# A tree of small networks, every leaf for every token, or the tokens sorted by leaf: one layer of an eight-layer kernel

## The reference, cut to what matters

```python
def _fff(x, node_w, node_b, w1, b1, w2, b2):       # once for q, k and v
    for _ in range(DEPTH):                          # DEPTH = 4
        score = einsum('nd,nd->n', xf, node_w[cur]) + node_b[cur]
        cur = 2 * cur + 1 + (score >= 0)
    leaf = cur - N_NODES                            # 0..15
    sel = one_hot(leaf, N_LEAVES)
    hidden_all = relu(einsum('nd,ldh->lnh', xf, w1) + b1[:, None, :])     # h is 64 wide
    hidden = hidden_all * sel.T[:, :, None]
    return einsum('lnh,lho->no', hidden, w2) + sel @ b2
attn = softmax(einsum('bqd,bkd->bqk', q, k) * scale)
out = einsum('bqk,bkd->bqd', attn, v)
```

## Time and profile before

| | us |
|---|---|
| median of 3 runs (1261.86 to 1264.03) | 1263.0 |
| the profiled execution's own time | 1262.16 |
| its span | 1260.3 |
| PE busy in the span | 1066.9 (85%) |
| DVE busy | 633.9 (50%) |
| ACT busy | 518.1 (41%) |
| POOL busy | 182.4 (14%) |

### The profile page before, as it was taken

The page is one execution under the profiler, slowest core; times in us unless marked ns, Lnnn a source line. Parts: engine busy times, 40 slices in busy tenths (PEclk is TensorE's granted clock), DMA queues, the critical chain, the costliest instruction groups (busy, mean ns, idle before and its releaser), DMA issues.

```text
span 1260.3 us, 12073 instructions
## 1 busy us (share of the span) xinstructions
PE 1066.9 (85%) x3752; PEld 460.1 (37%) x3752; DVE 633.9 (50%) x1123; ACT 518.1 (41%) x960; POOL 182.4 (14%) x160
## 2 busy tenths in 40 slices
PE   4898989898899999998847958677778999997677
PEld 2354545444222222222514633222224444442333
DVE  3213131332888778641513434799964555552443
ACT  4322222323367767675303435655552222226510
POOL 9000000000000000000173530366620000000000
PEclk9899999998799999998788979799997999999779
DMA  9600000020021212113013420000000000000001
GB/s 191 214 2 0 0 0 0 0 59 23 20 64 39 64 40 64 39 46 91 11 31 89 135 77 0 1 0 1 0 1 0 1 1 0 0 0 0 1 0 33
DMA packets 60307, 42.13 MB, mean 33 GB/s; under 512 B 17352, under 2 KB 57277, under 8 KB 60164
## 3 DMA queue, kind: packets, MB, share of 16 engines
q1 hardware_dynamic: 57956, 38.80, 11.3%
q0 software_dynamic: 2304, 2.76, 0.7%
HBM read 29.59 MB, written 13.67 MB: 34 GB/s over the span
## 4 chain that ended last, share of the span: by engine, by line
PE 61%; DVE 14%; issue 13%; ACT 8%; SPq 2%; DMA 1%; POOL 1%; DVEq 0%; ACTq 0%; POOLq 0%; another core or an unknown queue 0%
PE psum L566 59%; ACT sb_scr L1256 5%; DVE sb_scr L1736 3%; DVE sb_scr L1986 2%; DVE sb_scr L1995 2%; ACT psum L1256 1%; DVE sb_small L1697 1%; PE psum L1028 1%; SPq L347 1%; PE psum L1010 1%; DVE sb_x L1617 0%; DVE sb_h L1600 0%; ACT L1256 0%; DVE sb_scr L1638 0%; DVE sb_scr L1810 0%
## 5 line engine op out<-in xcount | busy, mean ns | idle before, releaser
L1256 ACT ACTIVATE sb_scr<-psum 128x512 f32<-128x512 f32 (+2 forms) x648 | 323.1, 537 | 491.9 <-PE psum L566 386.7
L566 PE MATMUL psum<-sb_h,sb_wide 128*128 (+1 forms) x448 | 226.4, 612 | 0.0
L1736 DVE TENSOR_REDUCE sb_scr<-psum 128x2 f32<-128x1024 f32 x128 | 154.3, 1223 | 43.7 <-PE psum L566 43.1
L566 PE MATMUL psum<-sb_scr,sb_wide 128*128 128x512 f32 x256 | 132.2, 598 | 6.1 <-DVE sb_scr L2057 6.1
L566 PEld LDWEIGHTS psum<-sb_h,sb_wide 128*128 128x128 f32 x448 | 86.0, 196 | 99.4 <-issue 99.0
L534 POOL DMA_INDIRECT expert_in<-sb_scr x32 | 31.2, 975 | 586.1 <-DVE sb_scr L1881 576.7
L1680 DVE TENSOR_SCALAR sb_scr<-psum,sb_b 128x512 f32<-128x512 f32 x48 | 36.0, 751 | 152.9 <-PE psum L566 152.9
L566 PE MATMUL psum<-sb_kstack,sb_qstack 96*128 96x512 bf16 x256 | 100.9, 406 | 6.4 <-DVE sb_scr L1736 6.0
L1256 ACT ACTIVATE sb_scr<-psum,sb_b 128x512 f32<-128x512 f32 x60 | 40.8, 687 | 159.2 <-PE psum L566 159.2
L566 PE MATMUL psum<-sb_qstack,sb_kstack 128*128 128x512 bf16 x256 | 99.1, 392 | 3.5 <-ACT sb_scr L1256 2.0
L566 PE MATMUL psum<-sb_wparts,sb_pick 96*128 96x512 bf16 (+1 forms) x192 | 66.4, 402 | 39.0 <-DVE sb_scr L1995 28.8
(11 more groups left out here) (222 smaller groups left out, 1299.8 us busy)
## 6 DMA issues: line engine op xcount, KB each, us to landing
sb_qstack<-q_bounce SPq DMA_DIRECT2D x48, 96.0 KB
sb_kstack<-k_bounce SPq DMA_DIRECT2D x144, 32.0 KB
expert_in<-sb_scr SPq DMA_DIRECT2D x4, 645.0 KB, 7.2
sb_scr<-expert_in SPq DMA_DIRECT2D x8, 322.5 KB
expert_out<-sb_scr SPq DMA_DIRECT2D x4, 512.0 KB, 5.9
sb_wide<-L_ffn_W SPq DMA_DIRECT2D x2, 1024.0 KB, 7.4
sb_scr<-expert_out SPq DMA_DIRECT2D x8, 256.0 KB, 4.7
q_bounce<-sb_scr SPq DMA_DIRECT2D x12, 128.0 KB, 2.4
```

Source lines behind the costliest of these rows:

```text
L566: return nc.tensor.matmul(out_, w, r, start=start, stop=stop, **kw)
L1256: return nc.scalar.activation(out_, in_, func, **kw)
L1736: v.reduce_max(headmax[:, g % 2, t:t + 2, j], banks, AX.X).then_inc(sem("maxed"), 1)
```

## The change

The first feed-forward is computed by leaf. Node scores for all 2048 tokens and three trees are taken at once, with tokens on partitions, and DVE works out each token's leaf, its place in a table sorted by leaf (each leaf's block padded to whole tiles of 128, so 32 tiles a tree), and for each tile the leaf it belongs to. POOL scatters the rows of h to the tables `leaf_in` in DRAM (16 indirect transfers a tree). Then 24 chunks of four tiles (8 a tree) go through: SP loads the rows of the chunk (`load_chunk`); SP (three) and ACT (one) load the weights of the tile's leaf, after reading the leaf's number from SBUF into a register (`value_load`); PE turns the rows, multiplies with w1 (64 wide) and with w2 (with b2 as a further row); ACT takes the relu, DVE copies, ACT stores the result to `leaf_out`. The rings of rows, results and weights hold four chunks each. POOL gathers the results back token by token (16 indirect transfers a tree). The attention is then a pipeline over all 16 steps, and the product that turns the probabilities has, in place of the identity, a diagonal matrix of the reciprocal sums (`inv_eye0`). `blank` has a buffer of its own, so the table of the fourth layer is cleared later; the parameter loads share one semaphore; the loops over batches are written out. The parts of the host's data layout: w1, w2, b1 and b2 of a leaf stand in one [128 x 193] block of `tree_rows`.

```diff
-            def trees(b, last):
...
-            with pe.Fori(0, NB - 1) as b:
-                trees(b, False)
-            trees(NB - 1, True)
+            def turn_rows(c):
+                pe.wait_ge(stacked[c % 4], 16 * (c // 4 + 1))
+                if c >= 2:
+                    pe.wait_ge(sem("xT_ready"), c - 1)
+                for j in range(CHUNK):
+                    m = nc.tensor.transpose(psum[:, c % 2, j * P:(j + 1) * P], x_rows0[:, c % 4, j, :], eye[:])
+                m.then_inc(sem("rows_turned"), 1)
+            def hidden_tiles(c):
+                pe.wait_ge(sem("xT_ready"), c + 1)
...
+                pe.wait_ge(w0_loaded[c % len(w0_loaded)], 16 * CHUNK * (c // len(w0_loaded) + 1))
+                for j in range(CHUNK):
+                    g = c * CHUNK + j
+                    m = mm(psum[leaf_side[j % 2], 2 + c % 2, j // 2 * P:(j // 2 + 1) * P], w_ring[:, g % W_RING, 0:LEAF_W],
+                           xT0[:, c % 2, j * P:(j + 1) * P], skip_group_check=True, tile_position=(0, j % 2 * LEAF_W))
+                m.then_inc(sem("hid0_done"), 1)
+            def out_tiles(c):
+                pe.wait_ge(sem("hid_ready"), c + 1)
...
+                m.then_inc(sem("tiles0_done"), 1)
+            for c in range(NCHUNK + 2):
+                if c >= 2:
+                    out_tiles(c - 2)
+                if c < NCHUNK:
+                    turn_rows(c)
+                if 1 <= c <= NCHUNK:
+                    hidden_tiles(c - 1)
             def attend(b, t):
                 pe.wait_ge(sem("probs0"), b * TT + t + 1)
...
                 for k in range(TT):
-                    m = nc.tensor.transpose(psum[:, (2, 6)[t % 2], k * P:(k + 1) * P], probs0[:, t % 2, k * P:(k + 1) * P], eye[:])
+                    m = mm(psum[:, (2, 6)[t % 2], k * P:(k + 1) * P], probs0[:, t % 2, k * P:(k + 1) * P], inv_eye0[:, t % 2, :],
+                           skip_group_check=True)
+            turn_qk(0)
+            for n in range(NT):
+                b, t = divmod(n, TT)
...
+                mm(bank(t % 2), qT0[b % 2][:, t * P:(t + 1) * P], kT0[b % 2]).then_inc(sem("scores0"), 1)
+                if (b, t) in beside:
+                    beside[b, t]()
+                if b >= 1 and t == 1:
+                    values_out(b - 1)
+                if n >= 1:
+                    attend(*divmod(n - 1, TT))
+```

In SP's program and in DVE's:

```diff
+            def load_leaves(c):
+                if c >= W_RING // CHUNK:
+                    sp.wait_ge(sem("tiles0_done"), c - W_RING // CHUNK + 1)
+                for g in range(c * CHUNK, c * CHUNK + CHUNK - 1):
+                    which = sp.value_load(leaf_at[0:1, g:g + 1], min_val=0, max_val=NTREE * LEAVES - 1)
+                    sp.dma_start(w_ring[:, g % W_RING, :], a["tree_rows"][g % 2][which]).then_inc(w0_loaded[c % len(w0_loaded)], 16)
+            for c in range(NCHUNK):
+                if c + 3 < NCHUNK:
+                    load_chunk(c + 3)
+                if c + W_RING // CHUNK < NCHUNK:
+                    load_leaves(c + W_RING // CHUNK)
+            shift(0)
+            for n in range(NT):
+                b, t = divmod(n, TT)
+                if n + 1 < NT:
+                    shift(n + 1)
+                normalize_probs(n)
```

More of the change, by code:

```diff
@@ L270, in build @@
         k_bounce = nc.dram_tensor("k_bounce", [HEADS, PARTS, DH, S], BF16, kind="Internal").ap()
+        leaf_in, leaf_out = ([nc.dram_tensor(f"leaf_{n}{f}", [SLOTS0, D], F32, kind="Internal").ap() for f in range(NTREE)]
+                             for n in ("in", "out"))
         expert_in = nc.dram_tensor("expert_in", [E1 * CAP, ROW], F32, kind="Internal").ap()
@@ L688, in out_of @@
[L688 to L696 removed]
+                        m = nc.tensor.transpose(psum[:, 3 + f, t * P:(t + 1) * P], tokens0[f][:, b * TT + t, :], eye[:])
@@ new lines, in _ @@
+            dve.wait_ge(sem("trees_loaded"), 16 * (2 + NTREE))
+            dve.wait_ge(sem("nodes0"), 1)
+            st = Steps("leaf_step", 0, 19)
+            HT = NT // 2
+            st.did(v.tensor_scalar(gates0.rearrange("p (k c) n -> p k (c n)", k=2), psum[:, 0:2, 0:HT * 48], 0.0, None, ALU.is_ge))
+            st.then(lambda: v.tensor_copy(reach0[0][:, :, 1], gates0[:, :, 0]))
+            st.did(v.tensor_scalar(reach0[0][:, :, 0], gates0[:, :, 0], -1.0, 1.0, ALU.mult, ALU.add))
+            for level in range(1, DEPTH):
+                here, of = reach0[level - 1], reach0[level].rearrange("p c (n two) -> p c n two", two=2)
+                st.then(lambda: v.tensor_tensor(of[:, :, :, 1], here, gates0[:, :, 2 ** level - 1:2 ** (level + 1) - 1], ALU.mult))
+                st.wait()
+                m = v.tensor_tensor(of[:, :, :, 0], here, of[:, :, :, 1], ALU.subtract)
+                if level < DEPTH - 1:
+                    st.did(m)
@@ L1709, in trees, with add_batch0, begin_cut_q @@
+            def add_batch0(b):
                 dve.wait_ge(sem("batch_out"), b + outs_before(FFN0) + 1)
                 add_to_x(b, 7)
-            go_right(0)
-            reach_leaves(0)
-            relu(0, 1)
-            with dve.Fori(0, NB - 1) as b:
-                trees(b, False)
-            trees(NB - 1, True)
+            def begin_cut_q():
+                for r in range(4):
+                    dve.wait_ge(gathered_sem[r], 16 * (NCHUNK // 4))
+                cut_q(0)
+            beside = {(2, 0): lambda: normalize_one(ATTN1, 0), (2, 1): begin_cut_q, (2, 2): lambda: cut_k(0),
+                      (3, 1): lambda: normalize_one(ATTN1, 1)}
@@ L1719, in values_by_token @@
+            shift(0)
+            for n in range(NT):
+                b, t = divmod(n, TT)
+                if n + 1 < NT:
+                    shift(n + 1)
+                normalize_probs(n)
+                if b >= 1 and t == 1:
+                    add_batch0(b - 1)
+                if (b, t) in beside:
+                    beside[b, t]()
+            normalize_one(ATTN1, 2)
+            add_batch0(NB - 1)
             def values_by_token(b):
```

625 lines of the change are left out of this document (361 added, 264 removed).

## The result

| | before | after |
|---|---|---|
| median, us | 1262.66 (1261.86 to 1264.03, 4 runs) | 1309.02 (1306.64 to 1315.78, 4 runs) |
| profiled execution's span | 1260.3 | 1305.7 |
| PE busy | 1066.9 (85%) | 969.3 (74%) |

The ratio is 1.0375, with a 95% interval of 1.0334 to 1.0416: slower by 3.75%, where 1.6% faster was forecast; the time lies above the range (1208 to 1292). PE has 98 us less to do and the kernel takes 46 longer. The same program ran again beside other runs of before: on one chip it took 1309.1 against 1261.8, on another 1235.9 against 1258.0 (which chip the first comparison ran on is not recorded). That difference between chips is half of this case, and the experiments come to it in their order.

The account below looks back on a forecast made before the run. PE's 512-column products were taken to bound three quarters of the layer. Routing, first scatter, 23 chunk periods and attention ended it at 296.4 us against 315.9, -19.5, giving 1243 us; range 1208 to 1292.

Parts of the forecast that it names:

- POOL, 96 x 1.275 = 122 us in all, is also below: Chunks: POOL's indirect transfers, 1.275 us each, stay below the chunk period and do not set it.
- Beside it SP fetches 12 weight blocks: First scatter, 21 us: SP's twelve fetches at 1.49 us each run beside POOL's scatters and end at 81.8 us.
- Routing, 17 us: Start of the layer: node products, gates, counting and handovers from 42.76 us, so POOL can start at 59.8.
- Register loads, 0.9 us: SP's weight fetches: a load from SBUF into a register, taken at 0.9 us between bounds 0.04 and 2.0.
- dear register loads: Rival: register loads up to 2.0 us make chunks 8.2 us, 1317 in all; gain gone at 1.33; chance 0.20.
- The chunk period, 5.6 us: Feed-forward chunks: 5.6 us from one to the next, 23 times, mostly at half clock; called the deciding term.
- SP's ring: Chunks: three fetches and one load of rows in SP's queue, 4.9 us a chunk.
- PE's and ACT's ring: Chunks: out tiles, relu and hidden tiles wait in turn, 3.65 us at full clock, 5.95 at half.
- half clock all through: Rival: PE at half clock in chunks (6.0 us) and attention (steps of 5.1 us), 1274 in all; chance 0.11.
- Attention, 77 us from the last result: From the last chunk's result at 219.4 us through copies, turns and attention to the layer's end at 296.4.
- The step of 3.3: Attention: the ring over PE's turn, scores and DVE takes 3.3 us a step against 2.31 before.
- DVE or POOL stalling each other: Listed among the things that would make the forecast wrong, without a size or chance of its own.

Follow-up runs that it names:

- e13: The changed kernel, unchanged, run a third time on another chip: 1235.9 us, ratio 0.9819 against the kernel before.
- e5: The kernel before plus 48 unused indirect scatters and 48 unused indirect gathers of 64 KB from POOL, back to back: 1337.1 us.
- e10: e5 again, unchanged, in the third set of runs: 1345.3 us.
- e1: The changed kernel with POOL's indirect transfers of k and v and all gathers spread over chunks and attention steps: 1265.9 us, ratio 1.0037 against before.
- e2: The changed kernel with the gathers of q and k held until the last chunk is stored: 1337.0 us.
- e4: The changed kernel with the attention order of the kernel before on DVE (maximum, then reciprocal, step by step): 1296.9 us, ratio 1.0257 against before.
- e7: The kernel before plus 48 + 48 unused plain transfers of 64 KB from POOL, in place of indirect ones: 1254.1 us.
- e8: The kernel before plus unused indirect transfers from POOL spaced one behind each hidden chunk, every 2.2 us: 1251.9 us.
- e17: The kernel before plus unused POOL transfers: 40 indirect back to back, 22 indirect spaced, 32 plain, one kind per batch: 1252.0 us.
- e6: The changed kernel with e1's spreading, e4's order and the fourth layer's table cleared later: 1214.5 us, ratio 0.966 against before.
- e12: e6 again, unchanged, in the third set of runs: 1230.4 us, ratio 0.9735 against before.
- e16: The kernel before with only the diagonal product of reciprocal sums added in the attention: 1251.7 us, ratio 0.9949 against before.
- e14: e7 again, unchanged, in the fourth set of runs: 1255.2 us.
- e3: The changed kernel with POOL's scatters held until the first 16 weight fetches have landed: 1253.2 us.
- e11: e3 again, unchanged, in the third set of runs: 1319.5 us.
- e18: The kernel before plus unused POOL transfers: 48 plain, 40 indirect with 128-byte rows, 40 indirect full-row, one kind per batch: 1256.0 us.

## Why the prediction was wrong

Times in us, the changed kernel's profiled executions in the first comparison and in e13:

| step | predicted | first comparison | e13 |
|---|---|---|---|
| POOL's first scatter | 59.8 | 62.3 | 67.0 |
| SP's twelfth fetch ends | 81.8 | 102.4 | 83.7 |
| PE's first chunk | 84.8 | 103.4 | 92.3 |
| DVE's first result | 90.6 | 131.2 | 99.1 |
| DVE's last result | 219.4 | 269.2 | 211.5 |
| `project_v` | 296.4 | 362.8 | 295.7 |

**The step that failed** in the first comparison is "POOL, 96 x 1.275 = 122 us in all, is also below", and with it the scatter "Beside it SP fetches 12 weight blocks": I priced POOL's transfers by POOL's own time alone, and took work beside them as hidden. Where the kernel was measured, they hold up whoever waits for PE, and SP. Against e13 that cost 37 us ahead of the first result (131.2 - 99.1, and the scatters had begun 4.7 earlier), 26 in the chunks (138.0 - 112.4) and 9 in the attention (93.6 - 84.1); 67 us with the 4.7 taken off, which is what `project_v` differs by. The experiments show that the transfers do it (e5 and e10, with nothing else changed, 76 and 84 us) and that spreading them saves 43 (e1). They do not show by what path, nor why some chips have it.

**Routing, 17 us**: 19.6 and 24.3. The clock was half for much of it (granted 0.73 between 42.7 and 62.3, 0.56 in e13), and I had summed it at full; the program is the same in both, and the lower grant goes with the longer time.

**Register loads, 0.9 us**: 0.27. The rival "dear register loads" gave a time near the measured one (1317) for a wrong reason. Its numbers fail at once: a fetch beside no POOL traffic is 1.1 us, not 1.49, and that rival needed a register load above 1.33.

**The chunk period, 5.6 us**: 4.9 with nothing held up (112.2 / 23 in e2, 112.4 / 23 in e13). SP's ring was too long by the register load: it measures 3.8 (131.20 to 135.03 in the first comparison, where SP had a chunk to catch up). So PE's and ACT's ring is left; it moves between 5.6 at half clock and 3.8 at full, where I had 5.95 and 3.65. The grant in e13's chunks was 0.50 to 0.76. The Trainium skill, TensorE: Matmul & The Clock Gate, section HAM oscillation, describes such a falling clock; the chunks agree, the attention does not (0.92, 0.89 and 0.92 in e13's windows from 214 to 292), so the case of half clock all through did not come.

**Attention, 77 us from the last result**: 84.1 in e13. The step of 3.3 was right (3.38), and so its cause (e4). Mis-sized were the things beside the steps and at the two ends: 15 intervals between maxima make 70.9 us, so 20 beyond 15 x 3.4, where I had 12.3 and 5 for the clock; start and tail make the other 13.2, where I had 9.9. Two of the intervals, with the second batch's value products, `project_q` and `project_k`, take 10.0 and 9.8 us.

**The whole**: -19.5 us forecast, -22.1 measured in e13 against the before beside it (1235.9 and 1258.0). There the sum came out right, but by luck: routing was +7, first scatter to first result +1, chunks -16, attention +7, so some 16 us each way. "No hold-up" was an assumption that I had not written down as one, and no chance stood for it but the general "DVE or POOL stalling each other".

Could the trace of before have shown it? Not by the earlier trace rows: those scatters run beside PE's shared feed-forward, and there DVE and ACT follow PE at once; but PE's work there ends after 17 of them, and in e5 20 had gone (48.2 to 73.0 us) before the first of PE's results was held up. Behind them, though, come the 40 transfers between products, and there the waits of before, 620 to 740 us, have these lines:

```profile
ACT sb_scr L1256 <- remote: 2.4, 2, 1.2
...
DVE sb_scr L1910 <- remote: 0.7, 1, 0.7
```

The same window of e7, e8 and e17 has none. In before 58 of PE's 143 increments there come over 0.2 us late, the latest 1.75 us. Small as they are, these waits were the sign of the hold-up in the very trace that I read, and I did not look there.

## What to carry to other kernels

Count a burst of indirect transfers as a possible cost to every engine that waits for PE, and to SP, for as long as it lasts; spread them behind the consumer's own progress (here two or three to a chunk). With that, with before's order of the steps and with the table cleared later, e6 is the best version on both kinds of chip (0.966 and 0.9735), though not free where the hold-up is: its three longest gaps between results are 8 us in e12 and 5.6 in e6. List the waits that nothing in the trace released, in the kernel before too: a few of them there were the first sign. They are no proof by themselves: e13 to e16 have some too, where only the record of the product is missing (in e14 at 66.1, 131.3 and 195.0 us, the same product of three batches that take no longer). Before believing a comparison of two kernels from different sets of runs, look at the level of the common kernel beside each: 6 us there was the sign of 66 us in e3 and e11. Putting the next step's maximum ahead of this step's reciprocal looks like a lead and was a longer ring (3.4 against 2.2 us).

## What the runs showed of the hardware

- On some chips, PE's increments reached waiting engines up to 15 us (changed kernel), 19 (e11) and 22 (e2) after the product's end while POOL issued indirect transfers every 1.25 to 1.27 us, and SP's fetch of a weight block took 3.0 us instead of 1.1. DVE's and ACT's increments were never over 0.2 us late in the same stretches. On other chips, the same programs showed nothing. What differs between them is open.
- One indirect transfer to an attention step cost nothing even there (e1: steps of 3.4 us). Whether plain transfers from POOL or narrower rows hold others up is open: e7, e14, e17 and e18 all ran where there was no hold-up.
- A register load from SBUF took 0.27 us, a whole fetch 1.13 from issue to issue; POOL's plain transfer occupied it 0.55 us (e7), its indirect one 0.94 to 0.97 and 0.3 between two.
